# Four chained layers on one core: the code search's maximum in two halves, layer 1's attention in 64-row blocks, swapped waits and a new order of steps

## The chip, the core and the metric

The kernel runs on one core of one Trainium2 chip. The metric is device time in microseconds (us), and the time before is 6159.45 us, the median of 3 runs (6157.94 to 6160.17). The engines are called PE (TensorE; PEld is its weight loads), DVE (VectorE), ACT (ScalarE), POOL (GpSimd) and SP (SyncE).

## What is computed

The input `x` is 16 images of 64x64 pixels with 256 channels. Four layers follow each other, each a group normalisation `_gn` over 32 groups, a layer on the result, and an addition to `x`:

```python
x = x + decode(argmin_k(|v|^2 + |e_k|^2 - 2 v e_k))            # v = _gn(x), 1024 codes
f, g, h = v @ Wf + bf, v @ Wg + bg, v @ Wh + bh                # v = _gn(x), 32, 32 and 256 columns
x = x + sigmoid(f_row @ g_row.T) @ h_row                       # per image row of 64 pixels
x0, x1, x2 = v @ w1, v @ w2, v @ w3                            # v = _gn(x), 4096 pixels
x = x + sigmoid(x2 @ softmax(outer(x0, x1), axis=0)) * v
x = x + layernorm(attention over channels of v @ w_qkv @ w_out)  # v = _gn(x), 4 heads
```

Layer 1's attention stays within a row of 64 pixels: its scores are 64x64 blocks.

## The kernel before

**Layout.** An image lives in SBUF as `XT`, channels on partitions (two halves `k` of 128), pixels along the free dimension. It is cut into 8 groups `g` of 512 pixels, each 4 tiles `u` of 128 pixels; a tile is two image rows. Values that need precision are split into an fp16 high and low part (`n_hi`, `n_lo`), and `split` makes three matmuls of each product.

**Three images at once.** A round of `images(B)` handles `new` (layers 0 and 1), `old` (layers 2 and 3) and `last` (the end of layer 3 and the output). There are 18 rounds for 16 images. In every round each engine has its own list of steps, written out (`fill(old, 0, 0); ...`), and the engines meet through semaphores alone. A `Step` is a counter: `after(im, i)` is the wait for item `i` to be made, `room(im, i, depth)` the wait until a buffer of that depth has a place. A queue takes its steps strictly in the written order, so a step that waits holds all that are behind it on its engine.

**Layer 2 (`old`)** makes 64 steps `h`. `fill(h, z)` on PE makes two matmuls of 12 rows in two row groups (L1175), `exp(h, z)` on ACT takes 128x1024 of them (L550), and `sums(h)` on PE makes four matmuls with 4 weight columns each in four column groups (L1184, fp32).

**Layer 0 (`new`), the code search.** For each of 32 tiles `t`, `score(t, half)` on PE makes six matmuls of 512 columns (L1021) into PSUM bank 5 + half. `best(t)` on DVE (L763) waits for both halves, adds the bias over 1024 codes and keeps the largest value in `m8`. `index(t)` on DVE (L768) looks the value up in the biased scores, `index(t)` on POOL gathers the code (L391), `turn0` on PE transposes two tiles (L1073), and `add0` (L774) and `stat1` (L749) on DVE add them and take the statistics. `score(t, 0)` waits until `best(t-1)` has let go of both banks (L1058).

```python
def best(im, t):
    dve.wait_ge(*l0_scored.after(im, t))
    dve.wait_ge(*l0_indexed.room(im, t, 2))
    v.tensor_tensor_reduce(biased[:, t % 2, :], bank(5, 2), e_bias[:, :], 1.0, -BIG, ALU.add, ALU.max,
                           m8[:, t % 2, 0:1]).then_inc(l0_maxed.sem, 1)
```

ACT makes the next group's normalised values and their high parts beside this (`l0_norm`, parts 0 to 3, L478 and L494), and POOL the low parts (L384).

**Layer 1 (`new`).** Per group: `l1_norm` (ACT L478 and L508, POOL L401), `l1_fg` (PE L1089, ACT L515 and L516), `l1_h` (PE L1021, DVE L783), `l1_scores` (PE L1109), `l1_tanh` (ACT L525, L530) and `l1_out` (PE L1119, DVE L790 and the statistics L749). `l1_scores` makes one 128x128 product of a tile with K = 32; the two diagonal 64x64 blocks are what is wanted. ACT copies them by tanh into `attn`, whose other blocks stay zero from the start, and adds one. `l1_out` multiplies 128x128 `attn` by `H`, fp32, four tiles for each channel half: 8 matmuls, of which the profile shows 16 records with 16 weight loads, for an fp32 matmul is two of each. Beside this run the end of layer 2 (`gate_chain`, `spread` L1202, `gating` L857, `gated_add` L407).

**Layer 3 (`old`)**: `l3_norm` (ACT, POOL L412), `l3_k`, `l3_qv`, `l3_kturn`, `l3_qturn`, `l3_ctx` on PE and their parts on ACT and DVE. Among them stand layer 2's preparation for `new`: `project`, `columns`, `extremes` (DVE, up to L828), `pieces` on POOL (L427 to L440) and `piece_turn` on PE; the next round's `fill(0, 0)` waits for these pieces.

## Time and profile before

| what | value |
|---|---|
| median of 3 runs | 6159.45 us |
| the profiled execution, its own time | 6152.6 us |
| its span | 6150.7 us |
| mean granted clock of PE, share of full | 0.952 |
| PE busy | 5617.3 us, 91% |
| DVE busy | 4166.6 us, 68% |
| ACT busy | 4097.9 us, 67% |
| POOL busy | 1926.0 us, 31% |
| one steady round (L763 starts at 2975.8 us and, in the next round, at 3341.1 us) | 365.3 us |
| a weight load of 128 fp32 columns in L1119, mean | 192 ns |

Busy time counts an instruction from its start to its end. Matmuls overlap each other, so that PE can be busy without being at its peak; the distance between two starts says more. An idle time before an instruction is put down to what released it.

### The profile page before, as it was taken

How to read it: one execution, taken by the hardware profiler on the slowest of the kernel's cores; microseconds unless marked ns; L12 is line 12 of the kernel's file. 1: busy time of each engine (PE TensorE's matmuls, PEld its weight loads, DVE VectorE, ACT ScalarE, POOL GpSimd, SP SyncE). 2: the span in 40 equal slices, each digit the busy share in tenths (PEclk: the TensorE clock that was granted, in tenths of full speed). 3: DMA queues.
4: the chain of work that ended last, by engine and by line, in shares of the span. 5: the costliest groups of instructions: out<-in, count | busy, mean ns of one | idle time of the engine just before them, and what ended most of it. 6: DMA issues, size and time to landing. Idle time of an engine off the chain costs nothing.

```text
span 6150.7 us, 103054 instructions
## 1 busy us (share of the span) xinstructions
PE 5617.3 (91%) x39656; PEld 2954.0 (48%) x39656; DVE 4166.6 (68%) x7691; ACT 4097.9 (67%) x6385; POOL 1926.0 (31%) x1588
## 2 busy tenths in 40 slices
PE   4789999999999999999999999999999999999976
PEld 2425537354463635536364453635446363553624
DVE  5547767676676767767676776767667676776715
ACT  1366757677675777757677675767757577675873
POOL 1214234242333424234242323424233342423412
PEclk8999999999999999999999999999999999999976
DMA  2000100201011020100101011010101102010000
GB/s 67 16 29 17 56 28 12 62 11 61 23 42 38 5 68 16 56 28 20 57 9 63 21 53 31 12 61 13 60 24 42 38 5 67 17 56 28 6 23 28
DMA packets 163125, 210.55 MB, mean 34 GB/s; under 512 B 13136, under 2 KB 146000, under 8 KB 162640
## 3 DMA queue, kind: packets, MB, share of 16 engines
q1 hardware_dynamic: 138064, 136.82, 6.9%
q0 software_dynamic: 24576, 67.14, 3.7%
q8 instruction: 319, 5.23, 0.3%
q14 instruction: 166, 1.36, 0.1%
HBM read 136.80 MB, written 67.11 MB: 33 GB/s over the span
## 4 chain that ended last, share of the span: by engine, by line
PE 55%; issue 23%; DVE 8%; ACT 7%; POOL 7%; SPq 0%; POOLq 0%; DMA 0%; DVEq 0%; ACTq 0%
PE PS L1021 26%; PE PS L1184 9%; PE PS L1175 4%; POOL quant_H L391 3%; PE PS L1119 3%; DVE work L763 2%; PE PS L1277 2%; POOL n_lo L384 2%; ACT big L550 2%; PE PS L1109 2%; PE PS L1050 2%; PE PS L1250 2%; DVE stats L749 1%; PE PS L1089 1%; PE PS L1134 1%
## 5 line engine op out<-in xcount | busy, mean ns | idle before, releaser
L550 ACT ACTIVATE big<-PS 128x1024 f32<-128x1024 f32 x2048 | 1997.7, 1023 | 1043.4 <-PE PS L1175 916.2
L1184 PE MATMUL PS<-big,w 128*4 128x512 f32 x8192 | 1117.1, 619 | 34.3 <-ACT big L550 34.3
L763 DVE CUSTOM_DVE_ANT_0 work<-PS,e_bias 128x1024 f32<-128x1024 f32 x512 | 626.7, 1224 | 740.2 <-PE PS L1021 740.2
L1021 PE MATMUL PS<-e_hi,n_hi 128*128 128x512 f16 x2048 | 781.6, 382 | 143.9 <-DVE m L763 104.5
L391 POOL DMA_INDIRECT quant_H<-emb_t,idx x512 | 487.4, 952 | 1263.0 <-DVE idx L768 1232.2
L1021 PE MATMUL PS<-e_lo,n_hi 128*128 128x512 f16 x2048 | 781.7, 382 | 0.0
L1021 PE MATMUL PS<-e_hi,n_lo 128*128 128x512 f16 x2048 | 779.8, 381 | 0.0
L1175 PE MATMUL PS<-rhs,lhs 12*128 12x512 bf16 x4096 | 595.9, 397 | 78.4 <-ACT big L550 53.8
L749 DVE BATCH_NORM_STATS2 stats<-XT 128x6 f32<-128x512 f32 x1024 | 651.5, 683 | 18.2 <-POOL XT L407 8.8
L768 DVE FIND_INDEX8 idx<-m,work 128x8 uint32<-128x1024 f32 x512 | 624.0, 1219 | 0.0
L1175 PEld LDWEIGHTS PS<-rhs,lhs 12*128 12x128 bf16 x4096 | 147.6, 91 | 895.9 <-ACT big L550 454.0
L449 POOL TENSOR_TENSOR rstd<-rstd,mhalf 128x4 f32<-128x4 f32 x128 | 129.2, 1009 | 1167.4 <-DVE rstd L946 1167.4
L1021 PEld LDWEIGHTS PS<-e_hi,n_hi 128*128 128x128 f16 x2048 | 199.9, 98 | 482.4 <-issue 274.7
L478 ACT ACTIVATE n_x<-XT,gt,gs 128x512 f32<-128x512 f32 x512 | 390.9, 804 | 46.7 <-DVE gt L744 45.8
L401 POOL TENSOR_TENSOR n_lo<-n_x,n_hi 128x1024 f16<-128x1024 f32 x128 | 272.6, 2130 | 324.0 <-ACT n_hi L508 321.5
L384 POOL TENSOR_TENSOR n_lo<-n_x,n_hi 128x1024 f16<-128x1024 f32 x128 | 273.1, 2134 | 296.1 <-ACT n_hi L494 295.1
L407 POOL TENSOR_TENSOR XT<-XT,big 128x1024 f32<-128x1024 f32 x128 | 299.6, 2359 | 152.0 <-DVE big L857 152.0
L494 ACT ACTIVATE n_hi<-n_x 128x512 f16<-128x512 f32 x256 | 150.2, 623 | 278.1 <-PE PS L1021 276.1
L1021 PEld LDWEIGHTS PS<-e_hi,n_lo 128*128 128x128 f16 x2048 | 200.8, 98 | 246.6 <-issue 7.6
L957 DVE SCALAR_TENSOR_TENSOR yout<-soft,rstd,PS 128x256 f32<-128x256 f32 x512 | 222.2, 475 | 136.7 <-PE PS L1277 106.6
L1021 PE MATMUL PS<-h_hi,n_hi 128*128 128x256 f16 x1024 | 293.7, 287 | 0.1
L1021 PE MATMUL PS<-h_lo,n_hi 128*128 128x256 f16 x1024 | 291.9, 285 | 0.0
(212 smaller groups left out, 10838.3 us busy)
## 6 DMA issues: line engine op xcount, KB each, us to landing
xin<-x SPq DMA_DIRECT2D x128, 512.0 KB, 3.9
out<-yout SPq DMA_DIRECT2D x128, 512.0 KB, 2.9
quant_H<-emb_t,idx POOLq DMA_INDIRECT x512, 2.7
XT<-emb SPq DMA_DIRECT2D x1, 1024.0 KB, 5.0
XT<-wh SPq DMA_DIRECT2D x1, 256.0 KB, 5.0
XT<-wqv SPq DMA_DIRECT2D x1, 256.0 KB, 5.3
XT<-wk SPq DMA_DIRECT2D x1, 128.0 KB, 5.2
w_sb<-w SPq DMA_DIRECT2D x1, 128.0 KB, 5.1
```

The source lines that it names most:

```text
L384: nc.gpsimd.tensor_tensor(n_lo[:, g % 2, :, :], n_x[:, g % 2, :, :], n_hi[:, g % 2, :, :], ALU.subtract).then_inc(l0_lo.sem, 1)
L391: nc.gpsimd.indirect_dma_start(quant[:, g % 2, u, :], None, emb_t, bass.IndirectOffsetOnAxis(ap=idx[:, t % (2 * GT), 0:1], axis=0),).then_ ...
L401: nc.gpsimd.tensor_tensor(n_lo[:, g % 2, :, :], n_x[:, g % 2, :, :], n_hi[:, g % 2, :, :], ALU.subtract).then_inc(l1_lo.sem, 1)
L407: nc.gpsimd.tensor_tensor(here, here, gated[:, g % 2, :, :], ALU.add).then_inc(g_added.sem, 1)
L478: return nc.scalar.activation(dst, XT[:, im % 2, k, g, :], copy, scale=gs[:, layer, k:k + 1], bias=gt[:, layer, k:k + 1])
L550: nc.scalar.activation(E[:, h % 2, z * 1024:(z + 1) * 1024], bank(2 * z, 2), ACT.Exp).then_inc(exped.sem, 1)
L749: last = v.bn_stats(stats[:, layer, k, g, :], XT[:, im % 2, k, g, :])
L763: v.tensor_tensor_reduce(biased[:, t % 2, :], bank(5, 2), e_bias[:, :], 1.0, -BIG, ALU.add, ALU.max, m8[:, t % 2, 0:1]).then_inc(l0_maxed. ...
L768: v.max_index(idx[:, t % (2 * GT), :], m8[:, t % 2, :], biased[:, t % 2, :]).then_inc(l0_indexed.sem, 1)
L1021: ins = mm(dst, a, b, start=first and j == 0, stop=last and j == 2)
L1175: ins = mm(bank(r), lhs[rr, t * P:(t + 1) * P], rhs[rr, f * GW:(f + 1) * GW], start=True, stop=True)
L1184: ins = mm(PS[32 * q:32 * q + 4, 4, :], w2[:, t, f, :], E[:, h % 2, q * 512:(q + 1) * 512], start=h == 0, stop=h == HALVES - 1, skip_group ...
```

## The change

Six things are changed.

1. The maximum of a tile is taken in two halves. `best(t, 0)` reads bank 5 only, `best(t, 1)` reads bank 6 and starts from the value that the first left in `m8`. `score` counts each half, and waits for the maximum of the same half of the tile before. There are 64 maxima of 512 elements instead of 32 of 1024.
2. `l1_scores` makes each 64x64 block by itself, with 64 weight columns and 64 moving columns, the second block in output partitions 64 to 127. `attn` is 64 wide and has no zero blocks. Tanh and the addition of one take all 128 partitions at once.
3. `l1_out` takes 64 rows at a time: block r = 0 from partitions 0 to 63 into bank 6, r = 1 from 64 to 127 into bank 7, and counts once for the group. DVE adds four pieces of 128x256 where it added two of 128x512.
4. Where a step has several waits, the order in which they are written is swapped in most functions: waits for room come first, waits for what is made come after.
5. `fill(0, 0)` has one more wait, for the last exponential of layer 3's k.
6. The lists of steps of all engines but SP are written anew. On PE the search of `new` now has 50 half-fills and 24 sums between its first and its last score where it had 47 and 23.

```diff
-        attn = sb("attn", [P, 2, GT, P])
+        attn = sb("attn", [P, 2, GT, ROW])
...
-        l0_scored, l0_maxed, l0_indexed = step("l0_scored", NT, 8), step("l0_maxed", NT, 1), step("l0_indexed", NT, 2)
+        l0_scored, l0_maxed, l0_indexed = step("l0_scored", 2 * NT, 16), step("l0_maxed", 2 * NT, 2), step("l0_indexed", NT, 2)
...
-        l1_outed, l1_added = step("l1_outed", 2 * NG, 4), step("l1_added", 2 * NG, 2)
+        l1_outed, l1_added = step("l1_outed", NG, 2), step("l1_added", 2 * NG, 2)
...
             def l1_fg(im, g):
+                act.wait_ge(*l1_scored.room(im, g, 2))
                 act.wait_ge(*l1_fged.after(im, g))
-                act.wait_ge(*l1_scored.room(im, g, 2))
...
             def l1_tanh(im, g):
+                act.wait_ge(*l1_outed.room(im, g, 2))
                 act.wait_ge(*l1_scored.after(im, g))
-                act.wait_ge(*l1_outed.room(im, 2 * g + 1, 4))
-                src = bank(4).rearrange("p (u n) -> p u n", u=GT)
-                for r in range(P // ROW):
-                    rr = slice(r * ROW, (r + 1) * ROW)
-                    last = nc.scalar.activation(attn[rr, g % 2, :, rr], src[rr, :, rr], ACT.Tanh, scale=0.5)
-                last.then_inc(l1_tanhed.sem, 1)
+                pairs = attn[:, g % 2, :, :].rearrange("p u i -> p (u i)")
+                nc.scalar.activation(pairs, PS[:, 4, 0:GT * ROW], ACT.Tanh, scale=0.5).then_inc(l1_tanhed.sem, 1)
                 act.wait_ge(*l1_tanhed.after(im, g))
-                for r in range(P // ROW):
-                    rr = slice(r * ROW, (r + 1) * ROW)
-                    last = nc.scalar.activation(attn[rr, g % 2, :, rr], attn[rr, g % 2, :, rr], copy, bias=ones[rr, 0:1])
-                last.then_inc(l1_attn.sem, 1)
+                nc.scalar.activation(pairs, pairs, copy, bias=ones[:, 0:1]).then_inc(l1_attn.sem, 1)
...
-            def best(im, t):
-                dve.wait_ge(*l0_scored.after(im, t))
-                dve.wait_ge(*l0_indexed.room(im, t, 2))
-                v.tensor_tensor_reduce(biased[:, t % 2, :], bank(5, 2), e_bias[:, :], 1.0, -BIG, ALU.add, ALU.max,
+            def best(im, t, half):
+                part = slice(half * 512, (half + 1) * 512)
+                if half == 0:
+                    dve.wait_ge(*l0_indexed.room(im, t, 2))
+                else:
+                    dve.wait_ge(*l0_maxed.after(im, 2 * t))
+                dve.wait_ge(*l0_scored.after(im, 2 * t + half))
+                v.tensor_tensor_reduce(biased[:, t % 2, part], bank(5 + half), e_bias[:, part], 1.0,
+                                       m8[:, t % 2, 0:1] if half else -BIG, ALU.add, ALU.max,
                                        m8[:, t % 2, 0:1]).then_inc(l0_maxed.sem, 1)
...
             def l1_out(im, g):
+                dve.wait_ge(*l1_outed.after(im, g))
                 for k in range(KC):
-                    here = XT[:, im % 2, k, g, :]
-                    dve.wait_ge(*l1_outed.after(im, 2 * g + k))
-                    v.scalar_tensor_tensor(out=here, in0=bank(7 - k), scalar=beta_c[:, k:k + 1], in1=here, op0=ALU.add,
-                                           op1=ALU.add).then_inc(l1_added.sem, 1)
+                    for r in range(2):
+                        here = XT[:, im % 2, k, g, :].rearrange("p (u r i) -> p u r i", u=GT, r=2)[:, :, r, :]
+                        made = PS[:, 6 + r, k * GT * ROW:(k + 1) * GT * ROW].rearrange("p (u i) -> p u i", u=GT)
+                        last = v.scalar_tensor_tensor(out=here, in0=made, scalar=beta_c[:, k:k + 1], in1=here, op0=ALU.add,
+                                                      op1=ALU.add)
+                    last.then_inc(l1_added.sem, 1)
...
             def score(im, t, half):
                 g, cols = t // GT, slice(t % GT * P, (t % GT + 1) * P)
+                pe.wait_ge(*l0_maxed.room(im, 2 * t + half, 2))
                 if half == 0:
                     pe.wait_ge(*l0_lo.after(im, g))
-                    pe.wait_ge(*l0_maxed.room(im, t, 1))
...
-                if half == 1:
-                    ins.then_inc(l0_scored.sem, 1)
+                ins.then_inc(l0_scored.sem, 1)
...
             def l1_scores(im, g):
                 pe.wait_ge(*l1_fgkept.after(im, g))
                 for u in range(GT):
-                    cols = slice(u % 2 * P, (u % 2 + 1) * P)
-                    ins = mm(PS[:, 4, u * P:(u + 1) * P], GTm[:, g % 2, u // 2, cols], FT[:, g % 2, u // 2, cols],
-                             start=True, stop=True)
+                    for r in range(2):
+                        cols = slice(u % 2 * P + r * ROW, u % 2 * P + (r + 1) * ROW)
+                        ins = mm(PS[r * ROW:(r + 1) * ROW, 4, u * ROW:(u + 1) * ROW], GTm[:, g % 2, u // 2, cols],
+                                 FT[:, g % 2, u // 2, cols], start=True, stop=True)
                 ins.then_inc(l1_scored.sem, 1)
 
             def l1_out(im, g):
+                pe.wait_ge(*l1_added.room(im, 2 * g + 1, 2))
                 pe.wait_ge(*l1_attn.after(im, g))
                 pe.wait_ge(*l1_hkept.after(im, min(2 * g + 2, 2 * NG - 1)))
-                pe.wait_ge(*l1_added.room(im, 2 * g + 1, 2))
                 for k in range(KC):
                     for u in range(GT):
-                        ins = mm(PS[:, 7 - k, u * P:(u + 1) * P], H[:, g % 2, u, k * P:(k + 1) * P], attn[:, g % 2, u, :],
-                                 start=True, stop=True)
-                    ins.then_inc(l1_outed.sem, 1)
+                        for r in range(2):
+                            rr = slice(r * ROW, (r + 1) * ROW)
+                            ins = mm(PS[:, 6 + r, (k * GT + u) * ROW:(k * GT + u + 1) * ROW],
+                                     H[rr, g % 2, u, k * P:(k + 1) * P], attn[rr, g % 2, u, :], start=True, stop=True)
+                ins.then_inc(l1_outed.sem, 1)
...
                     if im > 0:
+                        pe.wait_ge(*l3_kexped.after(im - 1, NG - 1))
                         pe.wait_ge(*l3_qsub.after(im - 1, NG - 1))
```

Of the lists, POOL's of layer 3 and the first steps of the search on PE and on DVE:

```diff
                 l3_norm(old, 0); l3_norm(old, 1); l3_norm(old, 2); gn(new, 2, 2); l3_norm(old, 3); l3_norm(old, 4)
-                project(new); l3_norm(old, 5); pieces(new); l3_norm(old, 6); l3_norm(old, 7)
+                project(new); pieces(new); l3_norm(old, 5); l3_norm(old, 6); l3_norm(old, 7)
...
-                fill(old, 32, 1); fill(old, 33, 0); score(new, 0, 0); score(new, 0, 1); sums(old, 32)
-                fill(old, 33, 1); fill(old, 34, 0); score(new, 1, 0); score(new, 1, 1); sums(old, 33)
+                fill(old, 32, 1); score(new, 0, 0); score(new, 0, 1); score(new, 1, 0); fill(old, 33, 0)
+                fill(old, 33, 1); score(new, 1, 1); sums(old, 32)
...
-                best(new, 4); add0(new, 0); index(new, 4); best(new, 5); index(new, 5); best(new, 6); add0(new, 1)
+                index(new, 2); best(new, 3, 0); best(new, 3, 1); index(new, 3); best(new, 4, 0); best(new, 4, 1)
+                add0(new, 0); index(new, 4); best(new, 5, 0); best(new, 5, 1); index(new, 5); best(new, 6, 0)
```

## Rows read from the trace of the kernel before

**Rows 1.** The page, section 1: busy us, share of the span, instructions.
```profile
PE 5617.3 (91%) x39656; PEld 2954.0 (48%) x39656; DVE 4166.6 (68%) x7691; ACT 4097.9 (67%) x6385; POOL 1926.0 (31%) x1588
```

**Rows 2.** Windows of one steady round: us, busy by engine, PEclk, DMA, GB/s.
```profile
2883.00:2973.00 90.00, 86.52 (x643) 35.23 (x642) 57.61 (x130) 79.34 (x139) 10.90 (x10) 0.93 0.30 94
2973.00:3106.00 133.00, 126.43 (x722) 46.43 (x724) 92.40 (x150) 64.18 (x76) 44.36 (x38) 1.00 0.10 31
3106.00:3121.00 15.00, 14.13 (x108) 3.55 (x106) 7.96 (x19) 13.43 (x15) 1.76 (x3) 1.00 0.06 19
3121.00:3200.00 79.00, 74.08 (x641) 62.35 (x634) 61.37 (x102) 68.07 (x121) 42.03 (x20) 0.96 0.00 1
3200.00:3248.00 48.00, 44.11 (x377) 34.37 (x375) 39.63 (x79) 30.68 (x51) 21.32 (x30) 1.00 0.01 2
```

**Rows 3.** Line L763, first image: ns min/median/max, first and last start; waiters.
```profile
L763 DVE CUSTOM_DVE_ANT_0 work<-PS,e_bias x32: 1223/1224/1225, 86.6 to 215.7; 128x1024 f32<-128x1024 f32 x32
...
  PE PS L1021: 37.8, 31
```

**Rows 4.** The same of the steady round, us 2973 to 3107.
```profile
L763 DVE CUSTOM_DVE_ANT_0 work<-PS,e_bias x32: 1223/1224/1226, 2975.8 to 3106.0; 128x1024 f32<-128x1024 f32 x32
...
  PE PS L1021: 4.4, 7
```

**Rows 5.** Timeline, all engines, us 3004.8 to 3007: start, us, engine, line.
```profile
3004.82 0.38 PE L1021 MATMUL PS<-e_hi,n_lo 128*128 128x512 f16 x1
...
3005.13 1.04 PE L1184 MATMUL PS<-big,w 128*4 128x512 f32 x8
3005.24 1.23 DVE L763 CUSTOM_DVE_ANT_0 work<-PS,e_bias 128x1024 f32<-128x1024 f32 x1 [0.72 <-PE PS L1021]
3005.30 0.63 ACT L494 ACTIVATE n_hi<-n_x 128x512 f16<-128x512 f32 x1 [5.22 <-PE PS L1021]
3006.10 0.10 PEld L1175 LDWEIGHTS PS<-rhs,lhs 12*128 12x128 bf16 x4 [0.86 <-issue]
...
3006.62 0.38 PE L1021 MATMUL PS<-e_hi,n_hi 128*128 128x512 f16 x1
...
3006.84 0.38 PE L1021 MATMUL PS<-e_lo,n_hi 128*128 128x512 f16 x1
```

**Rows 6.** Groups of DVE by line and shape, whole run: busy us, mean ns, idle before.
```profile
L957 DVE SCALAR_TENSOR_TENSOR yout<-soft,rstd,PS 128x256 f32<-128x256 f32 x512 | 222.2, 475 | 136.7 <-PE PS L1277 106.6 <-POOL rstd L449 30.1
...
L774 DVE TENSOR_TENSOR XT<-XT,PS 128x512 f32<-128x512 f32 x256 | 174.7, 683 | 66.9 <-PE PS L1073 66.9
```

**Rows 7.** Timeline of DVE, us 3013.4 to 3015.5.
```profile
3013.58 1.23 DVE L763 CUSTOM_DVE_ANT_0 work<-PS,e_bias 128x1024 f32<-128x1024 f32 x1 [1.13 <-PE PS L1021]
...
3014.92 1.22 DVE L768 FIND_INDEX8 idx<-m,work 128x8 uint32<-128x1024 f32 x1
```

**Rows 8.** Timeline of POOL, us 3196 to 3250.
```profile
3219.98 2.13 POOL L412 TENSOR_TENSOR o_lo<-xin,o_hi 128x1024 f16<-128x1024 f32 x1
3222.59 0.26 POOL L427 CAST pk<-s 128x96 bf16<-128x96 f32 x1 [0.48 <-DVE s L828]
...
3226.26 2.70 POOL L440 COPY work<-pk 128x384 bf16<-128x384 bf16 x3
```

**Rows 9.** Groups by line and shape, us 3121 to 3200 of the steady round.
```profile
L790 DVE SCALAR_TENSOR_TENSOR XT<-PS,beta_c,XT 128x512 f32<-128x512 f32 x16 | 11.8, 748 | 3.5 <-PE PS L1119 2.7
...
L530 ACT ACTIVATE attn<-attn,ones 64x256 f32<-64x256 f32 x16 | 8.1, 506 | 0.4
...
L525 ACT ACTIVATE attn<-PS 64x256 f32<-64x256 f32 x16 | 6.0, 378 | 2.8 <-PE PS L1109 2.6
```

**Rows 10.** Line L614: durations ns min/median/max, first and last start.
```profile
L614 ACT ACTIVATE soft<-PS x512: 374/383/413, 698.5 to 6139.9; 128x256 f32<-128x256 f32 x171
```

**Rows 11.** Timeline, us 2841.3 to 2842.1, weight loads of L1126.
```profile
2841.43 0.52 PEld L1126 LDWEIGHTS PS<-gt,w_sb 128*128 128x128 f32 x4 [0.77 <-DVE gt L744]
```

**Rows 12.** Line L493, a wait of the ACT queue.
```profile
L493 ACTq EVENT_SEMAPHORE  x128: 17/17/17, 75.6 to 5633.1; - x128
```

More of the change, by code:

```diff
@@ L1388, in _ @@
[L1388 to L1391 removed]
+                turn0(new, 4); score(new, 12, 1); score(new, 13, 0); score(new, 13, 1); fill(old, 43, 0)
@@ new lines, in _ @@
+                fill(old, 43, 1); sums(old, 42)
+                score(new, 14, 0); score(new, 14, 1); turn0(new, 5); fill(old, 44, 0); fill(old, 44, 1)
+                score(new, 15, 0); score(new, 15, 1); turn0(new, 6); score(new, 16, 0); score(new, 16, 1)
+                sums(old, 43)
+                fill(old, 45, 0); fill(old, 45, 1); score(new, 17, 0); score(new, 17, 1); turn0(new, 7)
+                score(new, 18, 0); score(new, 18, 1); score(new, 19, 0); fill(old, 46, 0); fill(old, 46, 1)
```

424 lines of the change are left out of this document (216 added, 208 removed).

## The prediction

> **What bounds the kernel now.** I read the page first: TensorE (PE) is busy for 91% of the span [rows 1]. That is no proof, because its matmuls overlap, so I cut one steady round of 365.3 us into stages [rows 2]. The granted clock is full in B, 0.93 in A and 0.96 in C; I expect no change there. Each round carries three images: the exponentials of layer 2 for `old` fill the work of the others. Stage A (fills 0 to 33, tails of `last`) has ACT busy 79 of 90 us and PE 87, B (the code search of `new`) has PE 126 of 133 and ACT only 64, the tail (last fills) has ACT 13.4 of 15, C (layer 1) has PE 74, ACT 68 and DVE 61 of 79, and D (layer 3) PE 44 of 48.
>
> B has the clearest pattern. Its 32 maxima start from 2975.8 to 3106.0, which is 4.20 us apart, and with no filler at all, in the first image, they start from 86.6 to 215.7, which is 4.16 us apart [rows 3, 4]. So filler isn't what paces B: a loop is. One tile's loop is 12 matmuls at 0.22 us, the last one's latency (0.38), the DVE's maximum over both banks (1.23), and 0.15 us until the next tile's first matmul [rows 5]: 11 x 0.215 + 0.38 + 0.04 + 1.23 + 0.15 = 4.17. PE waits 37.8 us for that maximum in the first image, and 4.4 us in a steady round [rows 3, 4], where filler covers the rest.
>
> **Search in two halves.** Score half 0 of tile t+1 now needs only half 0 of t's maximum, which runs beside score half 1. The loop is cut. What paces the stage is then the larger of PE's and DVE's work.
>
> DVE: a maximum over 1024 takes 1.22; over 512 elements a PSUM operation of DVE takes 0.68 [rows 6], so two take 1.37. From the maximum's start to the index's is 1.34 us [rows 7], so handing the value over costs 0.12, and the change adds one such hand-over. Per tile: 0.68 + 0.12 + 0.68 + 0.12 + index 1.22 + half an add (0.34) + a quarter of two statistics of much the same length (0.34) = 3.5 us; operations that follow each other overlap by some 0.07, so I take 3.4 with the waits below.
>
> First image, search alone: PE needs 2.58 + 0.22, DVE 3.4. Saved: 31 x (4.17 - 3.4) = **24 us**, once.
>
> Steady B, counted from the order written out for PE. Before: 64 score halves x 1.29 = 82.6, 47 fills x 0.215 = 10.1, 23 sums x 0.87 = 20.0 (0.98 to the next fill [rows 5], less 0.1 for the change of shape), 14 turn0 x 0.45 = 6.3 (four loads at 0.112, below), and 80 changes between steps that use the array in different shapes, at 0.1 each (from the last score matmul at 3004.82 to the sums at 3005.13 is 0.31, not 0.215 [rows 5]) = 8.0. Sum 127.0 of the 133 that pass. After: 82.6 + 50 fills 10.8 + 24 sums 20.9 + 6.3 + 66 changes 6.6 = 127.2, and I leave 1 us of waits. Saved: **5 us** a round (bounds: 1, if DVE with 32 x 3.4 = 109 us of work gets in the way in bursts; 6, if nothing waits). ACT and DVE have room: 64 and 92 us busy of 133 [rows 2].
>
> **Three half-fills move into B**: one from A, two from the tail. In the tail ACT has 15 instructions, nearly all exponentials, in 13.4 us [rows 2]: two fewer are 1.9 us. In A both engines are near full, so the third is worth 0.2 (PE) to 0.95 (ACT); I take 0.6. Saved: **2.5 us** a round. B hides them on ACT.
>
> **Other order.** Ten fewer shape changes in A (1 us of PE) are beside ACT's work, and steps swapped by a place or two there cost nothing by themselves. In D one move counts: on POOL the splitting `pieces(new)` now stands ahead of `l3_norm(old, 5)`. It runs from 3222.59 to 3226.26 + 2.70 = 3228.96, and group 5's low part, which was made at 3219.98, comes after it [rows 8], 9 us later at 3229. PE's k and qv of group 5 wait for that; kturn, qturn, ctx and two piece turns stand before them now, some 4 us of cover, and the fills of the next round get their pieces sooner. I take **+1 us** a round (bounds -2 and +5: 9 less 4).
>
> **Attention as 64-row blocks.** ACT: two tanh of 64x256 at 0.378 and two additions at 0.506 become one of each over 128x256. Time goes with the elements of a partition, not with partitions (128x256 costs the same 0.38 elsewhere [rows 10]), so 0.88 x 8 = 7.1 us of ACT go. DVE: two operations of 128x512 at 0.748 become four of 128x256, near 0.475 each [rows 6, 9]: +0.40 x 8 = +3.2 us, and it starts only when both halves of C are out. PE, output: 8 matmuls with 16 weight loads a group become 16 with 32. The stream of moving columns halves, but four loads of 128 fp32 columns, with one moving column each, take 0.52 us with the last one's latency (0.19 in the table), so 0.11 each [rows 11]: the loads alone pace it at 16 x 0.112 = 1.79, which is the time it takes now. Loads in different row groups do run side by side: the four of a fill take 0.10 together [rows 5]. So 16 pairs x 0.112 = 1.79, no change. PE, scores: 8 loads of 128 columns (0.90) become 16 of 64 columns in two column groups: 0.45 if side by side, 0.90 if not; I take 0.55, -2.8 us a round, less 0.6 for six more shape changes. C has PE, ACT and DVE all within 20% of its 79 us. With DVE up 3 and ACT down 7, I take **1 us** saved a round (bounds: +3, DVE's addition in full; -5).
>
> The Trainium skill (TensorEngine Tiling (Array Packing), Theoretical Speedup) gives up to 2x for a contraction of 64 rows or fewer. By it the output would take 0.9 us a group. Against it stands the pace of the loads, and I go by the row.
>
> **Late waits last.** Of two waits written before an instruction, the profile shows a separate semaphore instruction at the line of the second, as at L493, and none at the first, L492 [rows 12]. So the instruction itself carries the wait written first. After the score that ends at 3004.82 + 0.38 = 3005.20, DVE's maximum, whose first written wait it is, starts at 3005.24; ACT's copy, for which it is the second, at 3005.30 [rows 5]. Thus a late wait written last costs 0.06 more, not less. The change puts last the waits for the producer in most steps of C and D. Only where such a wait ends idle time does it cost: about two a group on the path, 8 groups, 0.06: **+1 us** a round (bounds 0 and +6). At the score it helps, since the maximum is now written first; that is in the 1 us left above. Each queue's next step is behind such a wait, so what follows is late by the same 0.06.
>
> **Sum.** 24 once; 15 rounds with search and exponentials x (5 + 2.5) = 112; 16 x 1 for attention; -16 for D's order; -16 for waits: 120 us. 6152.6 (profiled execution, span 6150.7) - 120 = 6032.6. That execution lies 6.9 under the median of the runs, 6159.45, so I predict 6040, 1.9% less.
>
> **Rivals.**
> *Given back (20%).* B ends sooner, but DVE, in order and 85% busy there, holds the scores, or D waits for POOL. For it: DVE rises to 109 of 128. Against it: 19 us are left. Half of the 112 goes: 6040 + 56 = 6096.
> *Attention gains (12%).* Layer 1 is bound by ACT and the chain fg, scores, tanh, output, and the output's pairs of loads overlap better than one load in 0.11 lets expect. 5 us a round rather than 1: 6040 - 64 = 5976. Against it: DVE gets more work. The Tiling rule of the Trainium skill would lead here.
> *Waits don't do what they say (10%).* Every swapped wait in C and D binds: 12 a group, 8 groups, 0.06 to 0.09: about 6 us a round, not 1: 6040 + 80 = 6120. Together with *given back* 6176, with half of it 6148: no change.
> *Slower (10%).* The fp32 weight loads of the two 64-row halves don't run side by side. Then the output takes 32 x 0.112 = 3.58 instead of 1.79 a group: 1.79 x 8 x 16 = +229, so 6269. It decides against the change once more than 52% of that (120 of 229) is on PE's path. For it: only bf16 loads are seen side by side, of 12 rows. Against it: those start within 0.1 us, and the four fp32 column groups of the sums run together [rows 5].
>
> **Numbers.** Forecast 48%, rivals 20, 12, 10 and 10. The range goes from 20 under the attention rival to 20 over the waits rival, 5955 to 6140; the slower one and combinations are left out. A measurement of this kernel tells 0.2% (12 us) from no change. Faster: 48 + 20 + 12 + half of the waits rival = 0.85; same: the other half, 0.05; slower 0.10.
>
> **What would show it.** First image: half-maxima pairs about 3.4 us apart instead of 4.17. Steady: 32 tiles in about 128 us, no wait of PE for the maximum over 1 us a round. Then two exponentials fewer after the last score, a maximum of 0.69 twice, round length near 359. Output: 32 loads in 1.8 us (right), 0.9 (attention rival) or 3.6 (slower). Waits: starts 0.10 instead of 0.04 after their releaser on DVE and ACT. The prediction is wrong if the tiles stay 4 us apart in the first image, or if C grows beyond 82 us.

## The result and the profile after

The changed kernel takes **5923.0 us** (median of 4 runs, 5916.35 to 5934.16), the kernel before beside it 6158.8: ratio **0.9619**, 95% interval 0.9601 to 0.9636. That is 3.8% less where 1.9% was forecast, and below the range's 5955. The profiled execution took 5934.16, its span is 5932.2.

The page, section 1, of the kernel after (against [rows 1]); the matmuls grew by 3072, all of them in the attention, and PE is busier in a shorter span:

```profile
PE 5488.0 (93%) x42728; PEld 2905.2 (49%) x42728; DVE 4208.7 (71%) x8970; ACT 3968.5 (67%) x6129; POOL 1920.9 (32%) x1588
```

Windows of one steady round of the kernel after. They are cut at the events A, B, tail, C, D (first exponential, first and last score matmul, last exponential, first `l3_k`), while [rows 2] end C later; read C and D there as one 127, here as 125:

```profile
2755.00:2845.00 90.00, 85.75 (x638) 34.85 (x637) 56.97 (x129) 79.87 (x140) 10.91 (x10) 0.91 0.29 94
2845.00:2968.00 123.00, 123.00 (x732) 47.95 (x730) 96.97 (x213) 64.58 (x77) 43.57 (x37) 0.99 0.11 33
2968.00:2981.00 13.00, 12.01 (x90) 3.23 (x92) 8.00 (x21) 10.74 (x12) 2.26 (x3) 1.00 0.07 21
2981.00:3047.00 66.00, 59.60 (x734) 49.89 (x728) 51.60 (x94) 52.90 (x92) 38.95 (x19) 0.97 0.01 2
3047.00:3106.00 59.00, 55.76 (x489) 42.99 (x485) 47.95 (x104) 39.28 (x65) 24.34 (x31) 1.00 0.01 2
```

PE is busy for all 123 us of B, where it was busy for 126 of 133. Busy time alone doesn't prove that the stage is PE's work, since matmuls overlap; e8 below tests it. Cut at the same events in every round, the 15 steady rounds have these means (us; each cell is worked out from the starts of those instructions):

| | to first exp | A | B | tail | C | D | round | last round |
|---|---|---|---|---|---|---|---|---|
| before | 325.7 | 88.1 | 133.4 | 14.1 | 70.3 | 59.4 | 365.3 | 345.2 |
| after | 301.2 | 89.1 | 123.2 | 12.9 | 67.9 | 58.7 | 351.7 | 354.9 |

So of 218.5 us, 24.5 are the first image's, 15 x 13.6 = 204 are the rounds', and the last round, which has no search to fill, gives 9.7 back. (218.5 is the difference of the two profiled spans; the medians differ by 235.8, because the profiled execution lies 6 us under the median before and 11 over it after.)

The new maximum by shape, whole run of the kernel after (columns: minimum, median and maximum in ns, first and last start):

```profile
L761 DVE CUSTOM_DVE_ANT_0 work<-PS,e_bias x512: 667/673/693, 84.4 to 5439.2; 128x512 f32<-128x512 f32 x171
L761 DVE CUSTOM_DVE_ANT_0 work<-PS,e_bias,m x512: 729/751/753, 86.1 to 5439.9; 128x512 f32<-128x512 f32 x171
```

The first half takes 0.67 us, near the 0.68 of the forecast; the second, whose starting value is an operand, takes 0.08 more. The attention, timeline of the kernel after around one group (start, duration, engine):

```profile
2996.41 1.86 PEld L1129 LDWEIGHTS PS<-attn,quant_H 64*128 64x128 f32 x32 [0.20 <-issue]
2996.41 2.00 PE L1129 MATMUL PS<-attn,quant_H 64*128 64x64 f32 x32
2998.47 1.66 DVE L791 SCALAR_TENSOR_TENSOR XT<-PS,beta_c,XT 128x256 f32<-128x256 f32 x4 [0.31 <-PE PS L1129]
2999.76 0.54 PEld L1117 LDWEIGHTS PS<-work 32*64 32x64 f32 x16 [0.21 <-issue]
2999.76 0.68 PE L1117 MATMUL PS<-work 32*64 32x64 f32 x16
```

Before, 16 loads and matmuls of the output took 1.86 and 2.05, and the scores 0.96 and 1.15:

```profile
3501.95 1.86 PEld L1119 LDWEIGHTS PS<-attn,quant_H 128*128 128x128 f32 x16 [0.20 <-issue]
3501.95 2.05 PE L1119 MATMUL PS<-attn,quant_H 128*128 128x128 f32 x16
3506.55 0.96 PEld L1109 LDWEIGHTS PS<-work 32*128 32x128 f32 x8 [0.21 <-issue]
3506.55 1.15 PE L1109 MATMUL PS<-work 32*128 32x128 f32 x8
```

32 loads pass in the time of 16: the two halves do run side by side, and each pair costs what one load of 128 fp32 columns costs. The rival on the slower side falls with this row.

### The profile page after: what moved, and what is told of

Read it like the earlier page. It is cut to its first block, busy times and chain, and to the rows that moved or that the text cites. A ratio compares the mean times of both kernels' runs of the same rounds, so it can differ in the third digit from the quotient of the medians.

```text
span 5932.2 us, 110733 instructions
## 1 busy us (share of the span) xinstructions
PE 5488.0 (93%) x42728; PEld 2905.2 (49%) x42728; DVE 4208.7 (71%) x8970; ACT 3968.5 (67%) x6129; POOL 1920.9 (32%) x1588
## 4 chain that ended last, share of the span: by engine, by line
PE 68%; DVE 15%; ACT 11%; issue 5%; POOL 1%; DMA 0%; SPq 0%; DVEq 0%; ACTq 0%; POOLq 0%
PE PS L1029 33%; PE PS L1195 12%; PE PS L1186 5%; ACT big L544 4%; DVE stats L743 3%; PE PS L1129 3%; PE PS L1080 2%; DVE XT L791 2%; PE PS L1288 2%; PE PS L1058 2%; ACT n_x L478 2%; PE PS L1261 1%; PE PS L1096 1%; ACT o_x L478 1%; DVE yout L959 1%
## 5 line engine op out<-in xcount | busy, mean ns | idle before, releaser
L544 ACT ACTIVATE big<-PS 128x1024 f32<-128x1024 f32 x2048 | 1994.9, 1024 | 1022.6 <-PE PS L1186 714.9
L1186 PE MATMUL PS<-rhs,lhs 12*128 12x512 bf16 x4096 | 549.0, 400 | 81.9 <-ACT big L544 61.9
L761 DVE CUSTOM_DVE_ANT_0 work<-PS,e_bias,m 128x512 f32<-128x512 f32 x512 | 383.7, 749 | 250.4 <-PE PS L1029 244.9
L761 DVE CUSTOM_DVE_ANT_0 work<-PS,e_bias 128x512 f32<-128x512 f32 x512 | 347.9, 679 | 265.2 <-PE PS L1029 264.6
L1186 PEld LDWEIGHTS PS<-rhs,lhs 12*128 12x128 bf16 x4096 | 135.0, 91 | 779.0 <-ACT big L544 451.4
L1195 PEld LDWEIGHTS PS<-big,w 128*4 128x4 f32 x8192 | 130.8, 85 | 366.9 <-issue 288.0
```

Source lines behind the costliest of these rows:

```text
L544: nc.scalar.activation(E[:, h % 2, z * 1024:(z + 1) * 1024], bank(2 * z, 2), ACT.Exp).then_inc(exped.sem, 1)
L761: v.tensor_tensor_reduce(biased[:, t % 2, part], bank(5 + half), e_bias[:, part], 1.0, m8[:, t % 2, 0:1] if half else -BIG, ALU.add, ALU.m ...
L1186: ins = mm(bank(r), lhs[rr, t * P:(t + 1) * P], rhs[rr, f * GW:(f + 1) * GW], start=True, stop=True)
L1195: ins = mm(PS[32 * q:32 * q + 4, 4, :], w2[:, t, f, :], E[:, h % 2, q * 512:(q + 1) * 512], start=h == 0, stop=h == HALVES - 1, skip_group ...
```

## The experiments

Each ratio is to the kernel before, run beside it on the same chip. On the chips of these runs the kernel before takes 6151.9 to 6159.8, so a difference of two medians that come from different chips is good to about 8 us. Means are of the 15 steady rounds of the profiled execution.

### One part alone in the kernel before

**e1_before_split**: the search in halves, the old order.

```diff
-            def best(im, t):
-                v.tensor_tensor_reduce(biased[:, t % 2, :], bank(5, 2), e_bias[:, :], 1.0, -BIG, ALU.add, ALU.max,
+            def best(im, t, half):
+                v.tensor_tensor_reduce(biased[:, t % 2, part], bank(5 + half), e_bias[:, part], 1.0,
+                                       m8[:, t % 2, 0:1] if half else -BIG, ALU.add, ALU.max,
...
-                best(new, 1); index(new, 1); best(new, 2); index(new, 2); best(new, 3); index(new, 3)
+                best(new, 1, 0); best(new, 1, 1); index(new, 1); best(new, 2, 0); best(new, 2, 1); index(new, 2)
```

> The kernel before with the maximum in two halves alone: order of steps, attention and wait order stay (the late wait is written first). Loop theory: before, the 32 tiles of the search are paced by score, whole maximum, score (4.17 us), and PE has some 10 us of waiting in each steady search, because two neighbouring half-fills run side by side and cost PE 0.22 together, not 0.43. Then the first search shortens by 24 us and each of 15 steady ones from 133 to about 124: 24 + 15 x 9 = 159, so 6000 us, ratio 0.974. Order theory: the gain came from the steps laid out anew, and the split alone gives the first search and 1 to 2 us a round: 6110 to 6120, ratio 0.993.

Measured: 6001.0, ratio 0.9742 (0.9726 to 0.9759). Means: to the first exponential 298.0, A 86.7, B 126.5, tail 14.4, C 69.7, D 59.5. Two thirds of the whole gain come from this edit alone, B 6.9 us a round.

**e2_before_attention**: `l1_scores`, `l1_tanh` and both `l1_out` of the changed kernel, nothing else.

> The kernel before with the 64-row attention alone (scores, tanh, output and DVE's four pieces). Theory: ACT's 7 us a round fall beside other work, PE's output keeps 1.8 to 2.0 us a group, the scores get 0.43 shorter, DVE gets 1.5 to 3 us more: 1 to 2.5 us a round, 6120 to 6143 us, ratio 0.994 to 0.997. Rival: layer 1 is bound by ACT and takes the whole 7 us: 6047, ratio 0.982.

Measured: 6140.1, ratio 0.9971 (0.996 to 0.9982): 18 to 20 us, against 16 forecast. C falls by 1.6, D grows by 1.0.

**e3_before_waits**: the waits in the new writing order.

> The kernel before with the swapped order of waits alone. Theory (the instruction carries the wait written first, another costs 0.06 more when it is late): in the search's loop the score gains 0.09 and the maximum loses 0.06, 0.03 x 31 x 16 = 15 us gained; in layers 1 and 3 one to two us a round are lost. In all between -5 and +30 us, ratio 0.999 to 1.005. Rival (a late wait written last is cheaper): at least 1 us a round gained in layers 1 and 3 too, 6130 or less, ratio 0.995.

Measured: 6167.7, ratio 1.0014 (1.0005 to 1.0024), +8 us against +16 forecast. But the prediction put its 16 into C and D, and there next to nothing happens: C falls by 0.6, D grows by 0.2. B grows by 1.2 (134.6), the tail by 0.5, and the first exponential comes 3.7 later. The expectation had the loop of the search gain by the swap; it loses, 4.20 us a tile in the first image against 4.17. The maximum, now with its late wait second, starts 0.14 us after the score's last matmul instead of 0.04. Timelines of e3, then of the kernel before:

```profile
103.42 0.38 PE L1021 MATMUL PS<-e_hi,n_lo 128*128 128x512 f16 x1
103.94 1.23 DVE L763 CUSTOM_DVE_ANT_0 work<-PS,e_bias 128x1024 f32<-128x1024 f32 x1 [1.64 <-PE PS L1021]
```

```profile
102.83 0.38 PE L1021 MATMUL PS<-e_hi,n_lo 128*128 128x512 f16 x1
103.25 1.22 DVE L763 CUSTOM_DVE_ANT_0 work<-PS,e_bias 128x1024 f32<-128x1024 f32 x1 [1.60 <-PE PS L1021]
```

**e15_before_pieces_first**: POOL's `pieces(new)` ahead of `l3_norm(old, 5)`.

```diff
-                project(new); l3_norm(old, 5); pieces(new); l3_norm(old, 6); l3_norm(old, 7)
+                project(new); pieces(new); l3_norm(old, 5); l3_norm(old, 6); l3_norm(old, 7)
```

> The kernel before with POOL's pieces(new) ahead of l3_norm(old, 5), nothing else. Theory of the prediction (PE's k of group 5 is late by it): +1 us a round, -2 to +5, so 6175 (6130 to 6240), D 60.4 instead of 59.4. Theory 'POOL's low part holds the small product on DVE': that product falls from 1.23 to 0.22 us, but the old order has PE's k of group 5 ahead of the piece turns, so both act: D within 1 us, sum 6140 to 6170. Rival 'early pieces pay here too' as in the new order: 6130 or less.

Measured: 6189.3, ratio 1.006 (1.0043 to 1.0076). D grows by 2.7 us a round, on the side and within the bounds that the prediction gave for this move, over the +1 taken. Part of it goes with the clock: D's granted clock is 0.97 in all rounds, in the kernel before it is 1.00 in ten of 15, and there a D at 0.97 takes 60.2 and one at 1.00 takes 59.0. The mechanism is the forecast one; PE waits 3 us for the low part before its k of group 5 (`--waits` of one D):

```profile
PE PS L1021 <- POOL o_lo L412: 3.0, 1, 3.0
```

DVE's product stays at 1.23 us (see e11 for why), and a later step of the same chain, L826, falls from 1.45 to 0.24.

### One part undone in the changed kernel

**e4_after_whole_maximum**: one maximum over 1024 again, in the new order (`best(im, t, 0)` returns, `best(im, t, 1)` takes both banks; the score's first half waits for it).

> The changed kernel with the maximum whole again: one over both banks after the second half score; the new order, attention and waits stay. Loop theory: the search goes back to about 4.14 us a tile, 133 us or more a round, and the first search to 129 + : 5923 + 24 + 15 x 10 = 6097 us, ratio to before 0.990. Order theory: the new order carries it, 5923 + 24 + 15 x 2 = 5977, ratio 0.970.

Measured: 6373.1, ratio 1.0347 (1.033 to 1.0364): both theories missed, by over 270 us. The window of B of one steady round of this kernel:

```profile
3451.00:3603.00 152.00, 126.65 (x733) 47.20 (x732) 92.32 (x150) 65.25 (x77) 43.51 (x37) 0.99 0.09 27
```

PE does the same work in 152 us as before in 133 [rows 2], with 25 idle, and all but 0.3 of that is waiting for the maximum:

```profile
PE PS L1026 <- DVE m L759: 25.1, 21, 1.4
```

The new order puts 18 or 24 score matmuls in a row in places and the fills between the halves of a tile; with the loop back, no filler stands where the loop leaves PE waiting. Filler covers a loop only at the place where it stands. The order was free to group the scores only because the loop was cut.

**e5_after_waits_back**: the producer's wait written first again in 26 places. The maximum is one of them, against what the expectation says; only the score keeps the new order. One of the places:

```diff
             def l1_tanh(im, g):
-                act.wait_ge(*l1_outed.room(im, g, 2))
                 act.wait_ge(*l1_scored.after(im, g))
+                act.wait_ge(*l1_outed.room(im, g, 2))
```

> The changed kernel with the waits written in the old order again (the producer's first, so that the instruction itself carries it), except at the maximum and at the score, which keep the new one. Theory 'as alone' (swapping the waits costs what it cost alone in the kernel before, 8 us): 5915 us, between 5900 and 5920, ratio to before 0.960. Rival 'tighter order, dearer waits' (in the new order more of these waits end idle time): 5885 or less. Rival 'the new writing order helps here': 5935 or more.

Measured: 5912.2, ratio 0.9603 (0.9587 to 0.9619), 11 us less than the changed kernel. The mechanism in two timelines, of the kernel after and of e5:

```profile
2991.30 0.68 PE L1117 MATMUL PS<-work 32*64 32x64 f32 x16
2992.09 0.38 ACT L523 ACTIVATE attn<-PS 128x256 f32<-128x256 f32 x1 [0.37 <-PE PS L1117]
```

```profile
2983.79 0.51 PE L1117 MATMUL PS<-work 32*64 32x64 f32 x11
2984.34 0.38 ACT L523 ACTIVATE attn<-PS 128x256 f32<-128x256 f32 x1 [0.28 <-PE PS L1117]
```

The scores end at 2991.98 and 2984.30; tanh starts 0.11 us after them with its late wait written last, 0.04 with it first. A steady round is 1.1 us shorter, 0.3 each in B, C and D.

**e6_after_attention_back**: the old attention in the new order.

> The changed kernel with layer 1's attention as whole 128-column tiles again, in the new order of steps. Theory 'a fixed worth' (20 us, as measured alone in the kernel before): 5943 us (5930 to 5955), C longer by about 1 us a round. Rival 'the new order needs it' (the new order places layer 1 by the costs of the new attention): 5975 or more, C longer by 3 us or more a round.

Measured: 5973.6, ratio 0.9701 (0.9684 to 0.9717). The attention is worth 51 us in the new order and 20 in the old: C grows by 4.3 a round, D falls by 1.2. The clock isn't behind it: the mean granted clock of C is 0.96 in e6 and 0.94 in the changed kernel. That is halfway between the 16 forecast and the 80 of the rival *attention gains*, and no run in the old order could show it.

**e7_after_order_back**: every engine's steps in the old order; split, attention and waits stay.

> The changed kernel with every engine's steps in the order of the kernel before (split search, new attention and new waits stay). Theory 'parts add': the split alone ran in 6001, attention gave 20, the waits cost 8, so 5989 us (5980 to 6000), and the order alone is worth about 65 us: B 126.6 instead of 123.2, tail 14.1 instead of 12.8, C longer by some 1 us, A shorter by 2. Rival 'the order adds nothing by itself, the parts multiply': 5945 or less. Rival 'the order is worth more than the split': 6050 or more.

Measured: 6020.9, ratio 0.9776 (0.976 to 0.9793). The parts don't add: in the old order, attention and waits on top of the split make it 20 us slower, not 12 faster, and the order is worth 98, not 65. Means: A 88.4, B 126.0, tail 14.1, C 69.2, D 60.5.

**e10_order_and_waits_back**: the same with the old writing order of waits too, so that it is e1 with the new attention. It also has the added wait of `fill(0, 0)`, which never binds there: the exponential that it waits for ends 4.5 us before the fill, in e10 as in e1.

> The kernel before with the split search and the new attention alone, that is the changed kernel with the old order of steps and the old writing order of waits. With the new waits it ran in 6020.9, the split alone in 6001. Theory 'the new waits cost 8 us here too, the new attention is what costs in the old order once the search is split': 6013 (6005 to 6018). Rival 'the waits cost more here': 5985 (5975 to 5995), that is the split's 6001 less attention's 20. The granted clock in A and C, 0.98 for the split alone and 0.93 to 0.95 with attention and waits, goes with the slower of the two.

Measured: 6082.6, ratio 0.9882 (0.9866 to 0.9899). Neither: 62 us slower than e7, though its late waits are the ones written first. And it is 82 slower than e1 (6001.0), from which only the attention tells it apart. So the attention takes off 20 us alone, costs 82 on top of the split in the old order with the old waits, and takes off 51 in the new order with the new waits; the swapped waits cost 8 alone and 11 in the new order, and take off 62 here. Windows of rounds of this one execution: C of a longer and of a shorter round (first two rows, 75 and 68 us), then 12 us at the same distance from the last exponential, of a longer round and of the shorter one, where they reach into D:

```profile
2331.00:2406.00 75.00, 67.95 (x746) 55.09 (x739) 51.57 (x94) 56.66 (x98) 41.26 (x20) 0.86 0.01 2
3429.00:3497.00 68.00, 60.52 (x742) 50.40 (x739) 51.55 (x94) 56.21 (x97) 40.01 (x20) 0.97 0.01 2
2030.00:2042.00 12.00, 11.14 (x90) 7.96 (x88) 5.73 (x12) 4.65 (x7) 4.25 (x2) 0.63 0.00 0
3492.80:3504.80 12.00, 10.63 (x118) 8.68 (x116) 9.35 (x20) 4.95 (x9) 3.65 (x2) 1.00 0.01 1
```

The same instructions (the x counts) take 7 us more at a mean granted clock of 0.86 than of 0.97: in the longer rounds part of C runs at the lower level, 1.2 instead of 2.4 GHz. Eleven of the 15 steady rounds are of the long kind (74.5 us). In the 12 us before, 2018 to 2030, in which the clock begins to fall (mean 0.81), PE was busy 9.88; in the short round at the same place it was busy 9.11 of 12, and the clock stayed at 1.00. So PE was not less busy before the fall, and why the clock falls in the one round and not in the other stays open. C's mean is 73.3 us at a granted clock of 0.88, against e7's 69.2 at 0.95: 15 x 4.1 = 62 of the 71 us between the two profiled spans (6090.0 and 6018.7).

**e11_after_pieces_later**: the reverse of e15, in the changed kernel.

> The changed kernel with POOL's pieces(new) behind l3_norm(old, 5) again, nothing else. Theory of the prediction (PE's k of group 5 waits for its low part, 4 us of cover, 9 us later): D 0.5 to 2 us shorter a round than the 58.7 of the changed kernel, sum 5895 to 5915. Rival 'covered': D within 0.3, sum 5915 to 5930. Rival 'the early pieces pay, since the next round's first fills read them': 5935 or more.

Measured: 5966.4, ratio 0.97 (0.9684 to 0.9716), 43 us slower; D 61.0 instead of 58.7 (60.3 in the rounds where the clock stays at 1.00, 62.0 to 62.3 where its mean is 0.97). Timelines of e11, then of the kernel after:

```profile
3452.85 0.28 DVE L824 TENSOR_REDUCE mt<-PS 2x1 f32<-2x128 f32 x1 [1.28 <-PE PS L1155]
3453.05 2.12 POOL L412 TENSOR_TENSOR o_lo<-xin,o_hi 128x1024 f16<-128x1024 f32 x1 [2.59 <-ACT o_hi L574]
3453.17 2.02 DVE L825 TENSOR_SCALAR dg<-ident,mt 2x2 f32<-2x2 f32 x1
```

```profile
3428.28 0.28 DVE L824 TENSOR_REDUCE mt<-PS 2x1 f32<-2x128 f32 x1 [1.28 <-PE PS L1155]
3428.59 0.22 DVE L825 TENSOR_SCALAR dg<-ident,mt 2x2 f32<-2x2 f32 x1
```

A product of four numbers takes 2.02 us when POOL's subtraction has started 0.12 us earlier, and both end together (3455.19 and 3455.17). It stands in the chain of layer 2's extremes, on which the pieces, the piece turns and the next round's fills hang, and PE's next step waits for it, 2.4 us here and 0.6 in the kernel after. The kernel before pays too, in two steps: its product ends with POOL's memset (3220.04 and 3220.03), and L826 ends behind the subtraction (3222.16 and 3222.11). Both are as long in nearly every round:

```profile
L823 DVE TENSOR_SCALAR dg<-ident,mt x16: 216/1232/1237, 311.8 to 5775.5; 2x2 f32<-2x2 f32 x16
L826 DVE TENSOR_SCALAR ma<-s,mx x16: 242/1448/1457, 312.7 to 5777.4; 128x32 f32<-128x32 f32 x16
```

```profile
3217.76 2.27 POOL L419 MEMSET work<- 128x2560 bf16 x1
3218.81 1.23 DVE L823 TENSOR_SCALAR dg<-ident,mt 2x2 f32<-2x2 f32 x1
3220.71 1.45 DVE L826 TENSOR_SCALAR ma<-s,mx 128x32 f32<-128x32 f32 x1
```

So e15, which moves the subtraction and not the memset, frees L826 and leaves the product. And POOL's move carries nearly the whole gain of the new order in D: 60.5 with all old (e7), 61.0 with all new but this (e11), 58.7 with it.

The Trainium skill (SBUF — State Buffer, "SBUF: two separate sides") says that GpSimd shares a pair of SBUF ports with those VectorE operations that run in a 2-port mode or have two inputs in SBUF (the latter only against a GpSimd operation that reads SBUF), as an exclusive lock: whichever starts first has it for its whole instruction, and the other one blocks. The trace agrees, with 2.02 against 0.22 and the two ends together; that POOL's memset, which reads nothing, holds the product too, speaks for the first kind, but no run here separates them.

### Who bounds B

**e8_after_fills_one_by_one** and **e9_before_fills_one_by_one**, the same edit in the changed kernel and in the kernel before:

```diff
-                    rr = slice(32 * r, 32 * r + PIECES)
+                    rr = slice(32 * (r % 2), 32 * (r % 2) + PIECES)
```

> The changed kernel with the row groups of the layer-2 fills taken modulo 2, so that two neighbouring half-fills use the same rows of the array and can't run side by side (the fills' products are those of the wrong row blocks, so the layer-2 output differs; the number, shape and place of all instructions are the same). Theory 'PE paces B, and a pair of half-fills side by side costs 0.215 us, not 0.43': B grows by some 24 pairs x 0.215 = 5 us a round, A by up to 4, the sum is 6000 to 6080 us. Rival 'the DVE or a loop paces B': B grows by less than 1.5 us a round, the sum is below 5970. Rival 'half-fills never ran side by side': no change in any step's pitch, 5923.

> The kernel before with the row groups of the layer-2 fills taken modulo 2 (the fills' products are those of the wrong row blocks, so the layer-2 output differs; nothing else changes). In the changed kernel the same edit made A 3.6 and B 4.9 us longer. Theory 'before, a loop paces B and PE idles 10 us of it': B grows by 0 to 2 us a round although PE gets some 22 pairs x 0.215 = 4.7 us more work there; A grows by some 3; sum 6190 to 6245 us. Rival 'PE paces B before too': B grows by over 4 us, A by 3, sum 6260 or more.

Measured: e8 6058.5, ratio 0.9838 (0.9822 to 0.9855), A +3.6, B +4.8; e9 6279.5, ratio 1.0211 (1.0185 to 1.0236), A +4.9, B +1.9, last round +12. Timelines of PE, of the kernel after, then of e8:

```profile
2853.08 0.40 PE L1186 MATMUL PS<-rhs,lhs 12*128 12x512 bf16 x4
2853.41 0.39 PE L1029 MATMUL PS<-e_hi,n_hi 128*128 128x512 f16 x1
```

```profile
2921.89 0.60 PE L1186 MATMUL PS<-rhs,lhs 12*128 12x512 bf16 x4
2922.43 0.39 PE L1029 MATMUL PS<-e_hi,n_hi 128*128 128x512 f16 x1
```

Four fill matmuls in four row groups take 0.33 us to the next step, in two row groups 0.54; a half-fill alone, two matmuls, takes 0.32 in B of the kernel before. So two neighbouring half-fills run side by side and cost 0.215 together. In B of the changed kernel there are 25 such pairs: 25 x 0.21 = 5.3, and B grows by 4.8, with PE busy 128 of 128. In B of the kernel before there are 20, in 9 of which the next score starts 0.51 us after the fill anyway, since it waits for the maximum; B grows by 1.9, not by 4. For B the first theories hit in both. The sum of e9 lies above its range because A, at a mean granted clock down to 0.80 in single rounds, and the last round took more than expected.

### Where the order's 98 us lie

**e13_new_search_old_layers** and **e14_old_search_new_layers**: on each engine the round's list is cut where layer 1 begins, and one part is taken from the old order, the other from the new.

> The changed kernel with the old order of steps in layers 1 and 3 (C and D) on every engine, the new one in A, B and the tail. All old it ran in 6021, all new in 5923. Theory 'mostly the search' (B 2.8 and the tail 1.2 us a round of the 6.6 that the two differ by, less 0.7 in A; C and D 3.1): 5970 (5955 to 5985), B 123.2, tail 12.9, C 69.2, D 60.5. Rival 'all in the layers': 6010 or more. Rival 'all in the search': 5935 or less.

> The reverse: the old order in A, B and the tail, the new one in C and D. Theory 'halves add' 5923 + 6021 - the run before = 5974 (5960 to 5990), B 126, tail 14.1, C 67.9, D 58.7. Rival 'all in the layers': 5935 or less. If the two don't add to within 15 us, the rest is the granted clock in A and C, which the rows then show (0.93 or 0.98 in A).

Measured: e13 6003.8, ratio 0.9759 (0.9742 to 0.9775); e14 5944.3, ratio 0.9661 (0.9645 to 0.9677). From all old (6021) the new order in C and D alone takes off 77 us, that in A, B and the tail alone 17; together 94 of the 98. (By the ratios, which allow for the other chip, 71 and 10, together 81 of 97.) My theory of halves is wrong by 30 us or more each way; "all in the layers" is nearest. The little that e13 gains is a net: its steady round is 2.5 us shorter than e7's (B -3.1, tail -1.3, A +1.7), and its last round, with no search in it, is 10 us longer (356.1 and 345.9). Means of e14: A 86.4, B 126.9, tail 14.1, C 67.0, D 58.7. Against e7, C and D are 4.0 shorter, and A is 2.0 shorter with the same steps; its mean granted clock is 0.965 against e7's 0.930. Windows of A, of a round of e14 and of a round of e10, whose steps stand in e7's order:

```profile
2412.00:2498.00 86.00, 81.48 (x642) 34.04 (x641) 57.70 (x130) 78.97 (x139) 10.92 (x10) 1.00 0.30 99
```

```profile
2102.00:2191.00 89.00, 85.46 (x641) 34.97 (x639) 57.48 (x129) 78.83 (x138) 10.90 (x10) 0.93 0.29 95
```

ACT's 79 us are the same; the granted clock is 1.00 and 0.93. The order of C and D changes the clock in the A that follows.

### A version that beats both

**e12_late_waits_first_old_end**, and the changed kernel and this version again on one chip (**e16_changed_again**, **e17_late_waits_first_old_end_again**):

```diff
             for new, old, last in images(B):
+                if new is not None:
...
+                else:
...
```

with the old order's steps behind `else`, e5's waits, and `f_sq` written first in DVE's `final_sq`.

> The changed kernel with the producer's wait written first (as in the run at 5912), final_sq's wait for the squares written first too, and in the last two rounds, which carry no new image, every engine's steps in the order of the kernel before. Theory 'the last round is slower in the new order by its order, since no search fills B': last round 346 instead of 351 to 355 us, sum 5906 (5900 to 5912). Rival 'it is slower by the clock of that execution alone': 5912 or more.

> The changed kernel as it is, for a comparison on one chip with the next. 5923 (5912 to 5934), ratio 0.962; last round 350 to 355 us in the profiled run.

> Late waits first and the old order in the last two rounds, once more. Theory: 11 us from the waits and 10 from the last round: 5902 (5893 to 5908), ratio 0.9590, last round 341 to 346 us, A to D of a steady round within 1 us of the changed kernel's. Rival 'the difference was the chip's': within 8 us of the run before.

Measured: e12 5900.0, ratio 0.9595 (0.9579 to 0.9611); e16 5928.3, 0.9633 (0.962 to 0.9646); e17 5904.5, 0.9595 (0.9582 to 0.9608). The version is 24 us (0.4%) below the changed kernel. Its last round takes 341 and 346 us, the changed kernel's 355 and 352.5. The stretch of the last round that holds only fills and sums, windows of the kernel after and of e12:

```profile
5660.00:5754.00 94.00, 75.00 (x378) 10.42 (x374) 0.00 (x0) 59.44 (x63) 0.00 (x0) 0.62 0.00 1
```

```profile
5636.00:5719.00 83.00, 65.02 (x378) 9.26 (x374) 0.00 (x0) 59.75 (x63) 0.00 (x0) 0.73 0.00 1
```

The same 378 matmuls take 11 us more. The granted clock is lower too, 0.62 against 0.73. The new order spaces the fills for a B that has scores between them, and here there are none; how the 11 us divide between this spacing and the clock wasn't separated. Nor were the late waits and the old end run apart on one chip: e5, with the waits alone, took 5912.2 on another.

## Why the prediction was wrong in size

The sign and several mechanisms stood; the forecast of 120 us became 236. Built up in this order, the parts are:

| part | forecast | measured | from |
|---|---|---|---|
| split in the old order | 24 + 15 x 5 = 99 | 159 | e1 |
| attention and waits on top of it | 16 - 16 = 0 | -20 | e7 against e1 |
| order of steps, half-fills and POOL's move in it | 15 x 2.5 - 16 = 22 | 98 | the changed kernel against e7 |

So of the miss of 116 us, 60 lie in the split and 76 in the order, and 20 go the other way. Neither of the prediction's own signs of being wrong came: the first image's tiles are 3.4 us apart, and C lasts 67.9. Term by term:

**First image, 24: right in the mean.** The first halves of its maxima start from 84.4 to 189.3, 3.39 us apart, and the first exponential comes 24.5 us sooner. In part this is luck: DVE isn't the steady pace of 3.4 that was assumed. It is busy for 96.0 of these 104.9 us, 3.1 a tile, single tiles are 2.4 to 5.6 apart, and the rest of the time it mostly waits for PE.

**Search, steady B, 5 a round: half.** B fell by 10.2, of which 6.9 by the split alone (e1). The step that failed is the count of PE's work in B: "47 fills x 0.215 = 10.1 ... Sum 127.0 of the 133 that pass". The fills of 128x512 in neighbouring row groups run side by side. [rows 5] had the hint, four loads of a fill in 0.10 us, and the prediction used it for the attention but not here. With 27 fill times instead of 47 the sum is 122.7, so by this count PE waited 10.7 us of 133.4, not 6. e8 and e9 show the price of a pair and that PE had the slack before and has none now. After the change B holds 121.8 us by the same count and lasts 123.2. The rival *given back* had DVE in the way; it is not, at 97 of 123.

**Three half-fills, 2.5 a round: less.** The tail fell by 1.2 instead of 1.9. A rose by 1.0 where it was to fall by 0.6; only part of that is the clock, since rounds with the same mean clock of 0.93 take 90.0 us after and 89.3 before.

**Attention, 16 in all: near it alone, 20 (e2), 51 in the new order (e6), and 82 us of loss between e1 and e10.** Of e2's 20 the steady rounds give 15 x 0.9 (C -1.6, D +1.0), and D's growth was not forecast. One price doesn't hold for all orders, which the prediction assumed. The output's loads pace it as forecast: it takes 2.00 us against 2.05. The Trainium skill (TensorEngine Tiling (Array Packing), Theoretical Speedup) gives up to 2x for it. In these rows the two halves do overlap, 32 loads in the time of 16, but that only makes up for there being twice as many, so that against the whole tiles the factor isn't there.

**Order, taken as +1 us a round for POOL's move and nothing elsewhere: this is the larger miss.** "Steps swapped by a place or two there cost nothing by themselves" was wrong in C and D: the order is worth 98 us with the half-fills, 77 of it in C and D with what follows in A. The price of POOL's move, +16, had the right sign and mechanism in the old order, where the move costs 36 us (e15), and the wrong sign in the new one, where undoing it costs 43 (e11). Two things failed in it. The cover: the prediction saw that two piece turns now stand ahead of group 5's k on PE and gave them and their neighbours 4 us of a delay of 9. In one D of the kernel after, the low part is ready 39.0 us after D's start, against 31.5 in e11, and k starts at 39.1 with no idle time of PE before it, so all of the delay is covered. And a term that it put at nothing: DVE's product no longer meets POOL's subtraction, which is worth 1.8 us on PE's path. Which of the moves in layer 1 gives C its 2 us wasn't tried.

**Waits, 16: right in sign alone (8, e3) and in the new order (11, e5), wrong in place.** A late wait written second does start its instruction later, 0.07 us on ACT's tanh and 0.10 on DVE's maximum. But the 8 of e3 lie in the search and not in C and D. And between e10 and e7 the same swap takes off 62 us, while C's granted clock rises from 0.88 to 0.95. The prediction had no term for that.

**"I expect no change" of the clock: wrong.** In A it is mostly 0.90 to 1.00 across kernels and rounds with the same work, worth some 4 us of a round, in C 0.86 to 0.98, worth up to 7. Changes in C and D move it, in A too (e14), and why wasn't found; part of what is put down above to an order, to waits or to the attention is this.

## What to carry to other kernels

A count of an engine's own work in a stage is worth as much as its cheapest step: look whether neighbouring steps overlap before dividing a stage into work and idle time, and test it by making that step dearer (if the stage grows in full, the engine bounds it; if not, a loop does). Moves on two queues are one edit: price a move on one queue against the order and the times that the other queues have after the change, look for what else it makes meet or part, and undo it in both settings, since 36 us slower and 43 us faster were the same line. A part's worth alone is no more than that: the same attention was worth 20, -82 and 51 us in three settings. An order of steps is fitted to its loops: after cutting one, lay the steps out anew, and expect the old loop to be far worse in the new order (6373).

## What the runs showed of the hardware

- A maximum whose starting value is an operand takes 0.75 us over 128x512, with a constant 0.67.
- A DVE product of 2x2 elements in SBUF takes 0.22 us, 2.02 when it starts behind a POOL subtraction of 128x1024, and 1.23 when it starts in the middle of a POOL memset of 128x2560; each time the two end together.
- Two fill matmuls of 12x128 by 512 columns take 0.32 us to the next step, four in four row groups 0.33, four in two row groups 0.54.
- 32 fp32 weight loads of 64x128, alternating between two halves of the rows, take 1.86 us, as 16 loads of 128x128 do; 16 of 32x64 take 0.54 where 8 of 32x128 take 0.96.
- The same instructions in the same stage take 68 or 75 us by the granted clock (0.97, 0.86), within one execution.
- ACT's tanh and DVE's maximum start 0.04 us after the matmul that they wait for when that wait is the one written first, and 0.11 and 0.14 when it is written second.
